# A decoder megakernel: one section per layer of its local-attention network, and 4-bit rounding from exponent bits

## The chip, the cores and the metric

The kernel runs on one core of a Trainium2 chip. The metric is the time of one execution on the device in microseconds (us); lower is better. The engines of a core are TensorE (PE; its weight loads are PEld), VectorE (DVE), ScalarE (ACT), GpSimd (POOL) and SyncE (SP), which issues DMAs.

## What is computed

Twelve stages in a row form a decoder: four layers of self-attention, cross-attention and a feed-forward part, on x of 4 x 256 tokens of width 128, all in float32. The change touches two of them.

The feed-forward part of layer 2 (`l2_ffn`) multiplies values that are rounded to a 4-bit grid in blocks of 16:

```python
_GRID = [0.0, 0.5, 1.0, 1.5, 2.0, 3.0, 4.0, 6.0]
_MID = [0.25, 0.75, 1.25, 1.75, 2.5, 3.5, 5.0]
scale = max(max(abs(xb)) / 6.0, 1e-12)           # over each block of 16
idx = searchsorted(_MID, abs(xb / scale))
q = _GRID[idx] * sign(xb) * scale
```

The last stage (`l3_ffn`) is a network of 6 layers of its own. Each layer shifts half of the channels by one token, projects to q, k and v for 16 heads of width 64, brings each head's q and k to unit length (a square, a sum over 64, a root, a reciprocal, a product), rotates them by position, attends within a local window (each block of 64 queries sees 96 keys at most), multiplies the heads by an output matrix and adds that; then follow a second shift, a layer norm and a gated feed-forward part.

## The kernel before

Every stage is a sequence of sections. A section (`nc.Block`) holds one program per engine, and at its end all engines wait for each other. Inside, engines are ordered by semaphores alone, and each engine works through its own program in the order written. A PSUM bank holds 128 x 512 float32. There are eight.

*The quantizer* (`quantize` in `l2_ffn`) is called twice, for a tile of 128 x 2144 (weights and tokens) and for one of 128 x 2816 (hidden values). ScalarE makes magnitudes and signs; VectorE then runs 14 instructions in a chain, each waiting for the one before: block maximum, scale, reciprocal, product, nine for the comparison with the seven midpoints, the doubling, and the sign (lines 1716 to 1723), and the product with the scale (line 1725).

*One pass of the layer loop* in `l3_ffn` (from line 1848) has these sections: transpose and shift; `project`; `local_attention`; the output product (`chunk_block` with the tag `heads_`, line 1884); the second shift; `norm`; the gated part.

`project` (line 1956) takes 16 steps u: 2 halves of the 1024 columns by 8 tiles of 128 tokens. In each, TensorE makes q, k and v, 128 x 512 each (lines 2012 and 2017; q and k go round six banks, v round two); ScalarE squares q and k into the two-deep buffer `squares` (2029; it shares its memory with `flat_p`, so the profile calls it `net_probs_turned`), takes the root of the step before (2034) and copies v (120); VectorE sums the squares (2059), takes the reciprocal of the step before (2064), guards this step's sum against zero (2068), and scales q and k of the step before into `unit` (2074). SP loads the layer's other weights and copies parts of v to `mid`. GpSimd has nothing to do.

`local_attention` (line 2076) works on 32 groups g (8 pairs of heads by 4 batches) in a software pipeline: GpSimd makes sine products (2152), TensorE transposes q and k and their sine products (2214, 2223), VectorE adds the two (2257, 2264), TensorE makes the scores on top of a window mask (2170, 2175), VectorE the maximum (2253), ScalarE the exponential with its sum (2237), GpSimd the division (2159), TensorE transposes (2188), VectorE copies (122), TensorE multiplies with the values (2203), ScalarE stores (120). On TensorE each turn of the loop is: scores of g, transposes of the probabilities of g-2, head products of g-3, transposes of g+3.

## Time and profile before

| | us |
|---|---|
| runs, median of 3 (lowest to highest) | 3107.61 (3104.6 to 3107.93) |
| profiled execution, own time | 3099.19 |
| its span | 3097.4 |
| TensorE busy | 2685.4 (87%) |
| VectorE busy | 1887.1 (61%) |
| ScalarE busy | 1459.9 (47%) |
| GpSimd busy | 993.8 (32%) |

The profile is one execution, with times counted from the span's start. The page gives sums over all twelve stages, which have different limits; a table of stretches or the timeline tells what one stage does. In the second pass of the layer loop `project` runs from about 2057 to 2108, the attention to about 2215, and the output product to 2231. The mean granted TensorE clock over the span is 0.937 of full speed.

### The profile page before, as it was taken

The numbers are of one execution on the slowest core, as the hardware profiler recorded it, in microseconds if no ns is written. First come the engines' busy times: TensorE is split into PE (matmuls) and PEld (weight loads), VectorE is DVE, ScalarE is ACT, GpSimd is POOL, SyncE is SP. The second block draws the span as 40 slices with busy tenths as digits, with TensorE's granted clock in tenths as the row PEclk, the third lists the DMA queues.
The fourth block names the chain that finished last, engine by engine and source line by source line (L and its number), as shares of the span: only waits on it lengthen the run. The fifth ranks groups of instructions, "written<-read, shape, count | busy, mean of one in ns | idle before, by whom it ended". The sixth has DMA issues, their size and how long they took to land. (4 is left out here: it accounts for less than half of the span.)

```text
span 3097.4 us, 61372 instructions
## 1 busy us (share of the span) xinstructions
PE 2685.4 (87%) x20645; PEld 1724.8 (56%) x20645; DVE 1887.1 (61%) x4110; ACT 1459.9 (47%) x4871; POOL 993.8 (32%) x1103
## 2 busy tenths in 40 slices
PE   5899969789899799672799979989989899899898
PEld 3555546456465465451455545746747647567376
DVE  3566656456577455557455558758578487486674
ACT  1455537227577365221355545445445355353543
POOL 0344425005366133000144423505306125043061
PEclk8899979899899899885899989999999999999999
DMA  2000000000000000000000011010010010100100
GB/s 65 1 0 0 0 8 2 26 19 2 4 1 2 30 0 0 5 8 0 26 1 0 0 49 28 2 53 12 22 42 2 30 34 2 49 15 22 42 2 28
DMA packets 42002, 49.32 MB, mean 16 GB/s; under 512 B 11963, under 2 KB 31301, under 8 KB 40838
## 3 DMA queue, kind: packets, MB, share of 16 engines
q1 hardware_dynamic: 41734, 45.89, 5.1%
q8 instruction: 151, 2.47, 0.3%
q14 instruction: 117, 0.96, 0.1%
HBM read 32.76 MB, written 0.52 MB: 11 GB/s over the span
## 5 line engine op out<-in xcount | busy, mean ns | idle before, releaser
L2152 POOL TENSOR_TENSOR net_sin_rows<-net_unit_qk,net_sin_table 128x512 f32<-128x512 f32 x192 | 243.1, 1269 | 680.4 <-SPq L2106 505.5
L2237 ACT ACTIVATE net_probs<-scores,net_negmax 128x96 f32<-128x96 f32 x768 | 251.7, 340 | 291.8 <-DVE net_negmax L2253 291.8
L1019 POOL TENSOR_TENSOR l_probs<-l_probs,rowinv 128x512 f32<-128x512 f32 (+2 forms) x256 | 192.3, 772 | 600.1 <-DVE rowinv L1031 599.3
L1039 DVE TENSOR_REDUCE negmax<-scores 128x1 f32<-128x508 f32 (+4 forms) x512 | 213.0, 468 | 221.7 <-PE scores L916 179.5
L1019 POOL TENSOR_TENSOR lora_probs<-lora_probs,rowinv 128x508 f32<-128x508 f32 (+1 forms) x256 | 149.5, 617 | 251.2 <-DVE rowinv L1031 251.2
L984 ACT ACTIVATE l_probs<-scores,negmax 128x512 f32<-128x512 f32 (+2 forms) x256 | 139.7, 552 | 166.9 <-DVE negmax L1039 166.2
L122 DVE COPY turned<-flip 128x512 f32<-128x512 f32 (+3 forms) x280 | 163.3, 583 | 74.1 <-PE flip L943 65.7
L2012 PE MATMUL bank<-net_w_qkv,xnT 128*128 128x512 f32 x384 | 199.6, 644 | 6.4 <-PEq L1848 6.4
L731 DVE TENSOR_REDUCE negmax<-scores 128x2 f32<-128x256 f32 (+2 forms) x192 | 157.8, 822 | 61.4 <-PE scores L639 34.9
L916 PE MATMUL scores<-kT,qM 64*128 64x512 f32 (+2 forms) x768 | 186.4, 562 | 9.1 <-ACT kT L120 4.7
L984 ACT ACTIVATE lora_probs<-scores,negmax 128x508 f32<-128x508 f32 (+1 forms) x256 | 117.9, 473 | 130.5 <-DVE negmax L1039 130.5
L2159 POOL TENSOR_TENSOR net_probs<-net_probs,net_inverse 128x384 f32<-128x384 f32 x192 | 158.2, 824 | 51.7 <-DVE net_inverse L2276 51.7
L2253 DVE TENSOR_REDUCE net_negmax<-scores 128x4 f32<-128x384 f32 x192 | 106.7, 556 | 105.0 <-PE scores L2175 105.0
L120 ACT ACTIVATE turned<-flip 128x512 f32<-128x512 f32 (+3 forms) x280 | 143.5, 513 | 56.9 <-PE flip L653 46.4
L966 PE MATMUL heads<-turned,V 128*64 128x256 f32 (+1 forms) x1280 | 166.3, 381 | 2.0 <-ACT turned L120 1.4
L2175 PE MATMUL scores<-net_qk_T 64*64 64x96 f32 (+1 forms) x3072 | 159.2, 243 | 0.0
L2214 PE MATMUL turn<-ident,net_unit_qk 128*128 128x128 f32 x768 | 129.7, 293 | 30.7 <-PEq L1973 30.7
L2237 ACT ACTIVATION_READ_ACCUMULATOR net_probs<-scores,net_negmax 128x1 f32 x768 | 156.1, 203 | 0.0
L2029 ACT ACTIVATE net_probs_turned<-bank 128x512 f32<-128x512 f32 x192 | 113.9, 597 | 81.8 <-PE bank L2012 81.8
L2175 PEld LDWEIGHTS scores<-net_qk_T 64*64 64x64 f32 x3072 | 123.0, 133 | 49.6 <-issue 49.6
L2264 DVE TENSOR_TENSOR net_qk_T<-turn,net_cos_T 128x512 f32<-128x512 f32 x192 | 132.8, 692 | 11.8 <-PE turn L2223 5.4
L716 POOL TENSOR_TENSOR cross_probs<-cross_probs,rowinv 128x1024 f32<-128x1024 f32 x64 | 119.8, 1893 | 61.6 <-DVE rowinv L726 61.6
(404 smaller groups left out, 6173.2 us busy)
## 6 DMA issues: line engine op xcount, KB each, us to landing
net_w_qkv<-in_L_ffn_Wqkv SPq DMA_DIRECT2D x7, 1536.0 KB, 6.2
net_vals_between<-net_vals SPq DMA_DIRECT2D x48, 192.0 KB, 2.5
net_w_out<-in_L_ffn_Wo SPq DMA_DIRECT2D x6, 512.0 KB
net_vals_between<-net_vals SPq DMA_DIRECT2D x48, 64.0 KB, 1.9
moe_w<-in_L_ffn_w13T SPq DMA_DIRECT2D x8, 256.0 KB, 2.7
net_w<-in_L_ffn_W SPq DMA_DIRECT2D x6, 341.0 KB
moe_w<-in_L_ffn_w2T SPq DMA_DIRECT2D x8, 128.0 KB, 2.3
ctx_tok<-in_ctx SPq DMA_DIRECT2D x1, 768.0 KB, 6.6
```

The lines of the kernel that those rows point to most:

```text
L122: return nc.vector.tensor_copy(dst, src)
L731: nc.vector.tensor_reduce(negmax[:, c:c + 2], scores[:, 2 * half:2 * half + 2, 0:nk], AX.X, ALU.max, negate=True).then_inc(maxed.sem, 1)
L916: last = nc.tensor.matmul(scores[:, 2 * qt + h, 0:nk], qM[rows, 0, t * P:(t + 1) * P], kT[rows, k0:k0 + nk], start=True, stop=cross)
L966: last = nc.tensor.matmul(heads[rows, q0 * P:QT * P], V[:, v0 + j, rows], turned[:, 2 * p + h, c0:c0 + w], start=(j == 0), stop=(j == part ...
L984: last = nc.scalar.activation(pr[:, slot(g, qt, h), k0:k1], scores[:, 2 * qt + h, k0:k1], ACT.Exp, bias=negmax[:, u * tail + w:u * tail + ...
L1019: last = nc.gpsimd.tensor_tensor(own, own, rowinv[:, u * tail + w:u * tail + w + 1].to_broadcast([P, k1 - k0]), ALU.mult)
L1039: last = nc.vector.tensor_reduce(negmax[:, u * tail + w:u * tail + w + 1], scores[:, 2 * qt + h, k0:k1], AX.X, ALU.max, negate=True)
L2012: nc.tensor.matmul(qk_bank(u, s), own, w_qkv[:, s * INNER + c * BANK:s * INNER + (c + 1) * BANK], start=True, stop=True).then_inc(filled.s ...
L2152: nc.gpsimd.tensor_tensor(halves(sin_rows[:, g % 2, :, :, :]), halves(tiles_of_group(g))[:, :, ::-1, :], sin_table[:, :, :, :, :].rearrang ...
L2159: nc.gpsimd.tensor_tensor(prob_blocks(g), prob_blocks(g), part, ALU.mult).then_inc(shared.sem, 1)
L2175: last = nc.tensor.matmul(scores[rows_of(h), g % 2, first:(w + 1) * KEYS], qk_T[rows_of(h), g % 3, 0, w * QB:(w + 1) * QB], qk_T[rows_of(h ...
L2237: last = nc.scalar.activation(prob_blocks(g)[:, w, :], score_blocks(g)[:, w, :], ACT.Exp, bias=maxima[:, g % 4, w:w + 1], accum_out=sums[: ...
```

## The change

The quantizer keeps the sign in the value. The value divided by the block's scale is masked to its exponent bits, which gives the power of two below it; that is held at 1 at least and multiplied by 1.5 x 2^22; adding and subtracting the result rounds the value to the grid's step. The sign instruction of ScalarE and its buffer go.

`project`, `local_attention` and the output product become one section, `attend`. k is copied from PSUM to `unit` by ScalarE; GpSimd squares it there and later scales it in place; q stays with ScalarE (square) and VectorE (scaling). The v products of TensorE and their copies follow three steps behind q and k. The attention's loops follow in the same programs, with waits for the units of a group (`wait_units`) before its sine products and its transposes, and with banks shared by hand. The output product is made in four parts, one per batch, behind the last groups; the wait for the layer's loads moves from VectorE's start of the attention to TensorE's first output part. ScalarE runs one small exponential ahead of the attention.

The removed loops of `project` and the loops of the attention that stay as they were are left out of the diff; both stand in the kernel above.

```diff
@@ quantize @@
-        STEPS = 14
-        step, side = signal("fp4_step", STEPS), signal("fp4_sign", 2)
+        STEPS = 9
+        step, side = signal("fp4_step", STEPS), signal("fp4_magnitude", 1)
         with nc.Block() as block:
             @block.scalar
             def _(act):
                 nc.scalar.activation(mag[:, 0:width], v, ACT.Abs).then_inc(side.sem, 1)
-                nc.scalar.activation(sgn[:, 0:width], v, ACT.Sign).then_inc(side.sem, 1)
             @block.vector
             def _(dve):
...
                 then(nc.vector.tensor_reduce(amax[:, 0:nb], blocks(mag), AX.X, ALU.max))
                 then(nc.vector.tensor_scalar(amax[:, 0:nb], amax[:, 0:nb], 1.0 / 6.0, 1e-12, ALU.mult, ALU.max))
                 then(nc.vector.reciprocal(inv[:, 0:nb], amax[:, 0:nb]))
-                then(nc.vector.tensor_tensor(blocks(mag), blocks(mag), of_block(inv), ALU.mult))
-                dve.wait_ge(side.sem, side.at(0, 2))
-                then(nc.vector.tensor_scalar(v, m, 5.0, 2.0, ALU.is_gt, ALU.mult))
-                then(nc.vector.scalar_tensor_tensor(v, m, 3.5, v, ALU.is_gt, ALU.add))
-                then(nc.vector.scalar_tensor_tensor(v, m, 2.5, v, ALU.is_gt, ALU.add))
-                then(nc.vector.tensor_scalar(v, v, 2.0, None, ALU.mult))
-                for mid in (1.75, 1.25, 0.75, 0.25):
-                    then(nc.vector.scalar_tensor_tensor(v, m, mid, v, ALU.is_gt, ALU.add))
-                then(nc.vector.scalar_tensor_tensor(v, v, 0.5, sgn[:, 0:width], ALU.mult, ALU.mult))
                 v3 = v.rearrange("p (n k) -> p n k", k=FP4_BLOCK)
+                then(nc.vector.tensor_tensor(v3, v3, of_block(inv), ALU.mult))
+                then(nc.vector.tensor_scalar(m.bitcast(I32), v.bitcast(I32), EXPONENT, None, ALU.bitwise_and))
+                then(nc.vector.tensor_scalar(m, m, 1.0, HALF_STEPS, ALU.max, ALU.mult))
+                then(nc.vector.scalar_tensor_tensor(v, v, 1.0 - 2.0 ** -24, m, ALU.mult, ALU.add))
+                then(nc.vector.tensor_tensor(v, v, m, ALU.subtract))
                 then(nc.vector.tensor_tensor(v3, v3, of_block(amax), ALU.mult))
                 assert done[0] == STEPS
...
@@ l3_ffn, layer loop @@
-        project(l, p, unit, vals, mid, mid_in, w_qkv, squares, norms, (sines, sin_table, cosines, cos_table, qk_rows, qk_cols),
-                loaded, (vec, w1, w2, w_out, GT))
-        local_attention(l, loaded, NLOADS, unit, vals, mid, mid_in, sin_table, cos_table, sin_rows, cos_T, qk_T, probs, flat_p,
-                        (maxima, sums, inverse), window16)
-        chunks = []
-        for t in (0, 4):
-            def outs(o, t=t):
-                for q in range(4):
-                    for c in range(PAIRS):
-                        last = nc.tensor.matmul(o[:, q * D:(q + 1) * D], unit[:, c, t + q, 0, :],
-                                                w_out[:, c, :], start=(c == 0), stop=(c == PAIRS - 1))
-                return last
-            chunks.append(Chunk("dve", outs, add_to(xin, t)))
-        chunk_block(chunks, n=l, iters=DEPTH, tag="heads_")
+        attend(l, p, unit, vals, mid, (sines, sin_table, cosines, cos_table, qk_rows, qk_cols), (sin_rows, cos_T, qk_T),
+               (squares, norms), (probs, flat_p, maxima, sums, inverse, window16), (loaded, NLOADS),
+               (vec, w_qkv, w1, w2, w_out, GT))
...
@@ attend (was project and local_attention) @@
+QK_BANKS, V_BANKS = (2, 3, 4, 5, 0, 1), (6, 7)
+TURN_BANKS, SCORE_BANKS, FLIP_BANKS, HEADS_BANK = (QK_BANKS[2], QK_BANKS[3], V_BANKS[0]), (QK_BANKS[4], QK_BANKS[5]), QK_BANKS[0:2], V_BANKS[1]
+OUT_BANKS = TURN_BANKS + SCORE_BANKS[0:1]
...
+    def wait_units(eng, g):
+        c, b = group(g)
+        for made in united:
+            eng.wait_ge(made.sem, made.at(l, c * D // BANK * NT + QT * (b + 1)))
...
@@ gpsimd @@
+        def make_sines(g):
+            if g >= 2:
+                pool.wait_ge(turned_sin.sem, turned_sin.at(l, g - 1))
+            wait_units(pool, g)
+            nc.gpsimd.tensor_tensor(halves(sin_rows[:, g % 2, :, :, :]), halves(tiles_of_group(g))[:, :, ::-1, :],
+                                    sin_table[:, :, :, :, :].rearrange("p t s h (f d) -> p (t s h) f d", f=2),
+                                    ALU.mult).then_inc(sined.sem, 1)
+        for u in range(STEPS + 1):
+            if u < STEPS:
+                pool.wait_ge(k_copied.sem, k_copied.at(l, u + 1))
+                if u >= 2:
+                    pool.wait_ge(added.sem, added.at(l, u - 1))
+                own = own_rows(unit, u, 1)
+                nc.gpsimd.tensor_tensor(by_pair(squares[:, u % 2, 1, :]), own, own, ALU.mult).then_inc(squared[1].sem, 1)
+            if u == STEPS:
+                pool.wait_ge(tabled.sem, tabled.at(l, 6))
+                make_sines(0)
+            if u >= 1:
+                own = by_head(own_rows(unit, u - 1, 1))
+                pool.wait_ge(norms_in.sem, norms_in.at(l, u))
+                nc.gpsimd.tensor_tensor(own, own, factors(u - 1, 1), ALU.mult).then_inc(united[1].sem, 1)
+        for s in range(1 - SINES, G + NORM):
             g = s + SINES
             if 0 <= g < G:
-                if g >= 2:
-                    pool.wait_ge(turned_sin.sem, turned_sin.at(l, g - 1))
-                nc.gpsimd.tensor_tensor(halves(sin_rows[:, g % 2, :, :, :]), halves(tiles_of_group(g))[:, :, ::-1, :],
-                                        sin_table[:, :, :, :, :].rearrange("p t s h (f d) -> p (t s h) f d", f=2),
-                                        ALU.mult).then_inc(sined.sem, 1)
+                make_sines(g)
...
@@ tensor @@
+        for u in range(STEPS + LATE_V):
+            if u < STEPS:
+                c, t = half_of(u)
+                for s, free in ((0, united[0]), (1, k_copied)):
+                    if u >= len(QK_BANKS) // 2:
+                        pe.wait_ge(free.sem, free.at(l, u - len(QK_BANKS) // 2 + 1))
+                    nc.tensor.matmul(qk_bank(u, s), xnT[:, t * P:(t + 1) * P],
+                                     w_qkv[:, s * INNER + c * BANK:s * INNER + (c + 1) * BANK],
+                                     start=True, stop=True).then_inc(filled.sem, 1)
+            v = u - LATE_V
+            if v >= 0:
+                c, t = half_of(v)
+                if v >= len(V_BANKS):
+                    pe.wait_ge(v_copied.sem, v_copied.at(l, v - len(V_BANKS) + 1))
+                nc.tensor.matmul(v_bank(v), xnT[:, t * P:(t + 1) * P], w_qkv[:, 2 * INNER + c * BANK:2 * INNER + (c + 1) * BANK],
+                                 start=True, stop=True).then_inc(v_filled.sem, 1)
...
+                wait_units(pe, g)
...
+            b = s - VALUES - LAST - 1
+            if b >= 0:
+                pe.wait_ge(stored.sem, stored.at(l, LAST + b + 1))
+                if b == 0:
+                    pe.wait_ge(loaded.sem, loaded.at(l, nloads))
+                    pe.wait_ge(rotated.sem, rotated.at(l, G))
+                    pe.wait_ge(exped.sem, exped.at(l, G))
+                for q in range(QT):
+                    for c in range(PAIRS):
+                        last = nc.tensor.matmul(out_bank(b)[:, q * D:(q + 1) * D], unit[:, c, QT * b + q, 0, :], w_out[:, c, :],
+                                                start=(c == 0), stop=(c == PAIRS - 1))
+                last.then_inc(out_made.sem, 1)
...
@@ scalar @@
+        for u in range(STEPS + LATE_V):
+            if u < STEPS:
+                act.wait_ge(filled.sem, filled.at(l, 2 * u + 1))
+                if u >= 2:
+                    act.wait_ge(added.sem, added.at(l, u - 1))
+                nc.scalar.activation(squares[:, u % 2, 0, :], qk_bank(u, 0), ACT.Square).then_inc(squared[0].sem, 1)
+                act.wait_ge(filled.sem, filled.at(l, 2 * u + 2))
+                copy("act", own_rows(unit, u, 1), by_pair(qk_bank(u, 1))).then_inc(k_copied.sem, 1)
+            if 1 <= u <= STEPS:
+                act.wait_ge(guarded.sem, guarded.at(l, u))
+                own = norms[:, (u - 1) % 2, :, :]
+                nc.scalar.activation(own, own, ACT.Sqrt).then_inc(rooted.sem, 1)
+            v = u - LATE_V
+            if v >= 0:
+                c, t = half_of(v)
+                act.wait_ge(v_filled.sem, v_filled.at(l, v + 1))
+                copy("act", vals[:, t, c * BANK:(c + 1) * BANK], v_bank(v)).then_inc(v_copied.sem, 1)
+        nc.scalar.activation(primer[:, :], ones[:, 0:1], ACT.Exp).then_inc(primed.sem, 1)
...
@@ vector @@
+        for u in range(STEPS + 1):
+            if u < STEPS:
+                for made in squared:
+                    dve.wait_ge(made.sem, made.at(l, u + 1))
+                if u >= 2:
+                    for made in united:
+                        dve.wait_ge(made.sem, made.at(l, u - 1))
+                nc.vector.tensor_reduce(norms[:, u % 2, :, :], squares[:, u % 2, :, :].rearrange("p s (h d) -> p s h d", d=DH),
+                                        AX.X, ALU.add).then_inc(added.sem, 1)
+            if u >= 1:
+                own = norms[:, (u - 1) % 2, :, :]
+                dve.wait_ge(rooted.sem, rooted.at(l, u))
+                nc.vector.reciprocal(own, own).then_inc(norms_in.sem, 1)
+            if u < STEPS:
+                own = norms[:, u % 2, :, :]
+                dve.wait_ge(added.sem, added.at(l, u + 1))
+                nc.vector.tensor_scalar(own, own, 1e-24, None, ALU.max).then_inc(guarded.sem, 1)
+            if u >= 1:
+                dve.wait_ge(norms_in.sem, norms_in.at(l, u))
+                nc.vector.tensor_tensor(by_head(own_rows(unit, u - 1, 0)), by_head(by_pair(qk_bank(u - 1, 0))), factors(u - 1, 0),
+                                        ALU.mult).then_inc(united[0].sem, 1)
...
+        for b in range(B):
+            own = xin[:, QT * b:QT * (b + 1), :]
+            dve.wait_ge(out_made.sem, out_made.at(l, b + 1))
+            nc.vector.tensor_tensor(own, own, out_bank(b).rearrange("p (t d) -> p t d", t=QT), ALU.add).then_inc(out_added.sem, 1)
```

## Rows read from the trace of the kernel before

**Rows 1.** The page: busy time, share of the span and instructions of each engine.
```profile
PE 2685.4 (87%) x20645; PEld 1724.8 (56%) x20645; DVE 1887.1 (61%) x4110; ACT 1459.9 (47%) x4871; POOL 993.8 (32%) x1103
```

**Rows 2.** Projection, mid-attention: us; PE, PEld, DVE, ACT, POOL busy (count); clock, DMA, GB/s.
```profile
2057.00:2108.40 51.40, 46.30 (x96) 17.82 (x96) 45.03 (x86) 31.40 (x65) 0.00 (x0) 0.93 0.23 62
2125.30:2197.30 72.00, 72.00 (x944) 57.84 (x943) 58.15 (x116) 38.54 (x208) 47.27 (x46) 1.00 0.01 2
```

**Rows 3.** Timeline, start of the projection: start, length, engine, line, operation [idle before <-releaser].
```profile
2060.87 0.60 ACT L2029 ACTIVATE net_probs_turned<-bank 128x512 f32<-128x512 f32 x1 [1.11 <-PE bank L2012]
...
2061.94 0.60 ACT L120 ACTIVATE net_vals<-bank 128x512 f32<-128x512 f32 x1 [0.47 <-PE bank L2017]
...
2062.80 0.60 ACT L2029 ACTIVATE net_probs_turned<-bank 128x512 f32<-128x512 f32 x1 [0.26 <-PE bank L2012]
...
2064.29 1.22 DVE L2059 TENSOR_REDUCE net_qk_norms<-net_probs_turned 128x16 f32<-128x1024 f32 x1 [1.36 <-ACT net_probs_turned L2029]
```

**Rows 4.** Timeline, one steady step of the projection.
```profile
2073.13 1.22 DVE L2059 TENSOR_REDUCE net_qk_norms<-net_probs_turned 128x16 f32<-128x1024 f32 x1
...
2074.27 0.24 DVE L2064 RECIPROCAL net_qk_norms<-net_qk_norms 128x16 f32<-128x16 f32 x1
...
2074.43 0.13 DVE L2068 TENSOR_SCALAR net_qk_norms<-net_qk_norms 128x16 f32<-128x16 f32 x1
...
2074.55 1.29 DVE L2074 TENSOR_TENSOR net_unit_qk<-bank,net_qk_norms 128x512 f32<-128x512 f32 x2
...
2075.29 0.30 PEld L2012 LDWEIGHTS bank<-net_w_qkv,xnT 128*128 128x128 f32 x2 [0.79 <-DVE net_unit_qk L2074]
```

**Rows 5.** Timeline, last sum of squares, GpSimd's first sines, first window product.
```profile
2103.99 1.22 DVE L2059 TENSOR_REDUCE net_qk_norms<-net_probs_turned 128x16 f32<-128x1024 f32 x1
...
2108.48 3.79 POOL L2152 TENSOR_TENSOR net_sin_rows<-net_unit_qk,net_sin_table 128x512 f32<-128x512 f32 x3 [84.91 <-SPq L2106]
...
2113.25 0.33 PE L2170 MATMUL scores<-net_window,ident 128*128 128x384 bf16 x1
```

**Rows 6.** GpSimd's groups by shape, two of them.
```profile
L2152 POOL TENSOR_TENSOR net_sin_rows<-net_unit_qk,net_sin_table 128x512 f32<-128x512 f32 x192 | 243.1, 1269 | 680.4 <-SPq L2106 505.5 <-PE turn L2223 174.8
...
L1019 POOL TENSOR_TENSOR l_probs<-l_probs,rowinv 128x512 f32<-128x512 f32 x128 | 130.3, 1039 | 445.4 <-DVE rowinv L1031 445.4
```

**Rows 7.** Timeline, hand-overs from VectorE to GpSimd to TensorE.
```profile
2208.96 0.18 DVE L2276 RECIPROCAL net_inverse<-net_sums 128x4 f32<-128x4 f32 x1 [0.87 <-ACT net_probs L2237]
...
2209.22 0.83 POOL L2159 TENSOR_TENSOR net_probs<-net_probs,net_inverse 128x384 f32<-128x384 f32 x1 [1.26 <-DVE net_inverse L2276]
...
2210.10 0.42 PEld L2188 LDWEIGHTS flip<-ident,net_probs 128*128 128x128 f32 x4 [0.18 <-POOL net_probs L2159]
```

**Rows 8.** TensorE's queue: a separate wait (ns), and idle time before head products.
```profile
L2220 PEldq EVENT_SEMAPHORE  x186: 51/51/51, 1901.9 to 3035.4; - x186
...
2126.68 0.20 PEld L2203 LDWEIGHTS heads<-net_probs_turned,net_vals 128*64 128x64 f32 x4 [0.17 <-issue]
```

**Rows 9.** Timeline, last head products, last copy, output products, last addition.
```profile
2211.44 0.44 PE L2203 MATMUL heads<-net_probs_turned,net_vals 128*64 128x128 f32 x4 [0.68 <-ACT net_unit_qk L120]
...
2214.73 0.38 ACT L120 ACTIVATE net_unit_qk<-heads 128x256 f32<-128x256 f32 x1 [0.85 <-PE heads L2203]
...
2215.42 14.53 PE L1884 MATMUL bank<-net_w_out,net_unit_qk 128*128 128x128 f32 x128 [0.73 <-PEq L2106]
...
2229.99 0.69 DVE L490 TENSOR_TENSOR xin<-xin,bank 128x512 f32<-128x512 f32 x1 [6.46 <-PE bank L1884]
```

**Rows 10.** Timeline, the quantizer's rounding steps, first and last of both calls.
```profile
1389.51 1.28 DVE L1716 TENSOR_SCALAR fp_inputs<-fp_mag 128x2144 f32<-128x2144 f32 x1
...
1409.11 2.39 DVE L1725 TENSOR_TENSOR fp_inputs<-fp_inputs,fp_amax 128x2144 f32<-128x2144 f32 x1
...
1437.90 1.63 DVE L1716 TENSOR_SCALAR fp_hid<-fp_mag 128x2816 f32<-128x2816 f32 x1
...
1463.11 3.09 DVE L1725 TENSOR_TENSOR fp_hid<-fp_hid,fp_amax 128x2816 f32<-128x2816 f32 x1
```

345 lines of the change are left out of this document (168 added, 177 removed).

## The prediction, made before the changed kernel ran

> **What bounds the kernel now.** I read the page first: TensorE is busy for 87% of the span, no other engine for more than 61% [rows 1]. That average covers twelve stages, and the change touches two places, so the stretches of those decide. The table by stretch of the layer loop's second pass (of six) [rows 2] shows two regimes. In the projection (51.4 us) VectorE is busy for 45.0 us and TensorE for 46.3 us at a mean clock of 0.93; in the middle of the attention (72.0 us) TensorE is busy all the time at the full clock and VectorE for 58.2 us. So in the attention a TensorE instruction costs its time, and work of the others is hidden.
>
> The timeline of one projection step [rows 4] says who sets the pace: VectorE starts the sum of squares at 2073.13, the reciprocal 1.14 us later, the guard 0.16 after that, the two scalings 0.12 after that, and the next sum 1.39 later: 2.81 us with no hole. TensorE waits 0.79 us for a scaling to free a bank. From the sum of step 1 at 2064.29 [rows 3] to that of step 15 at 2103.99 [rows 5] there are 14 periods in 39.70 us, 2.84 each. GpSimd does nothing in this stretch. In the 4-bit quantizer [rows 10] VectorE runs alone, one instruction after another, each waiting for the last: all of it is on the path.
>
> **The quantizer.** Between the normalization by the block maximum and the last product stand now two one-input instructions and seven with two inputs. For the 2144 wide call they fill 1389.51 to 1409.11, 19.60 us; for the 2816 wide one 1437.90 to 1463.11, 25.21 us. Two one-input and two two-input instructions replace them. One-input ones take 1.28 and 1.63 us, two-input ones 2.39 and 3.09 us, each with some 0.03 between: 2 x 1.31 + 2 x 2.42 = 7.5 us and 2 x 1.66 + 2 x 3.12 = 9.6 us. Saved: 12.1 + 15.6 = 27.8 us. The mask on integers isn't in the trace. If it ran at the two-input pace it would cost 1.1 and 1.5 us more (saved 25.2); a gain below the one-input row is not to be had for as many elements. I take the row of the same kind, 27.8. The sign on ScalarE ran beside VectorE's first reduction: worth nothing.
>
> **The projection, step by step.** VectorE loses one scaling of two (about 0.65 us), so by itself it would need some 2.2 us a step; TensorE would then be next, with 46.3 / 16 = 2.9 us a step at 0.93 of the clock (2.7 at the full one). But the new order makes a ring through two engines. GpSimd issues in program order: square k(u), wait for the reciprocal of u-1, scale k(u-1), square k(u+1). VectorE issues: wait for both squares of u, sum(u), and only then the reciprocal of u-1. So the square of u releases the sum of u, behind it comes the reciprocal of u-1, that releases the scaling of u-1, and behind this waits the square of u+1. None of the four overlaps another. Double buffers don't help, since it is queue order that ties them. The period is:
> - sum to reciprocal, start to start: 1.14 [rows 4];
> - reciprocal 0.24 [rows 4] and the hand-over to GpSimd 0.08 (reciprocal ends 2209.14, GpSimd starts 2209.22) [rows 7]: 0.32;
> - scaling 128x512 on GpSimd with a factor repeated over 64 elements: the nearest row is the scaling of 128x512 probabilities by a repeated factor, 1.04 [rows 6];
> - square 128x512: not in the trace as such. Bounds: 1.04, the row with a repeated operand, and 1.27, the row with two full 512 wide operands [rows 6]. It reads two full streams (the same one twice): I take 1.27;
> - hand-over back: 0.05, as from GpSimd to TensorE (2210.05 to 2210.10) [rows 7].
>
> Sum 3.82 us a step, against 2.84. Guard, q's scaling (done 2.1 us after the sum's start), ScalarE's square, copy, root and copy (some 2.0 us) and TensorE's products lie inside it: bank waits are for step u-3 and k is copied before it is wanted, so they have over 1 us to spare. 14 periods take 53.5 instead of 39.7 us: +13.8 per pass. With the square at 1.04 the period is 3.59 and the price 10.6; with both at 1.27 it is 4.05 and 17.0. A sum gets three waits more on VectorE's queue, a few hundredths, left to the range.
>
> The Trainium skill (GPSIMD Engine Reference, section 3.1) gives a GpSimd instruction with two inputs about 2.6 cycles per element and dispatch on top, and section 4.1 says to keep elementwise work on VectorE. The rows agree for two full operands but show 1.04 for a repeated one; if the page's rule held for the scaling too, the time would be 6 x 3.2 = 19 us above my sum. By both the work moved is dearer where it lands.
>
> **Start of the projection.** k's first copy ends at 2061.47. Value products go behind, so k1 takes the place that q1 has now (2062.80) [rows 3]: copied at 2063.40, squared from 2063.48 to 2064.75, sum of step 1 at 2064.80 instead of 2064.29: +0.5 (+0.3 with the quicker square).
>
> **The seam to the attention.** Now the first window product of the scores comes at 2113.25, 9.26 us after the last sum's start (2103.99) [rows 5]; the barrier holds everybody until 2108.48, then GpSimd makes three sine products in 3.79 us. New, counted from that sum: scaling of k14 ends at 1.14 + 0.32 + 1.04 = 2.50, sines(0) at 3.77, scaling of k15 at 4.81, sines(1) at 6.08, sines(2) at 7.35, its turn and the window product at about 7.85. Gain 1.4. The last value product waits for ScalarE and is over by about 4 us, so TensorE isn't late. If TensorE is slow here, the gain is 0.9. Loading the exponential's table earlier gains nothing: ScalarE waits there for the first scores anyway.
>
> **The attention itself.** The instructions are the same. TensorE gets two more waits for every group (q and k of the group's tiles), with the group's transposes queued behind them and VectorE and ScalarE behind those. They are satisfied long before, but a wait of its own on that queue takes 0.051 us, and before the head products there is a hole of 0.17 us at such a place [rows 8]. As TensorE has no idle time there [rows 2], I take 2 x 0.051 = 0.10 us for 28 groups: +2.8 per pass. Bounds: 0, if the queue runs ahead, and 0.17, or 4.8 per pass. GpSimd's two extra waits per group are hidden by its idle time.
>
> **The end of the attention.** Now TensorE waits between the last groups and for the barrier, then makes the output product in 14.53 us from 2215.42, and the addition ends at 2230.68 [rows 9]. New, the four parts stand between the last groups: after the head products of group 29 (2211.44 to 2212.1) come three group pieces of 0.6 and the four parts, 16.3 us, to 2228.45, and a half-size addition of about 0.5 to 2229.0. Gain 1.7; bounds 0 (the parts wait for ScalarE's copies) and 2.0. What is late next is TensorE itself. SP issues the same DMAs in the same order; the wait for the layer's loads moves from VectorE to TensorE, 100 us after they were issued, so it costs nothing.
>
> **Sum.** Per pass +0.5 + 13.8 - 1.4 - 1.7 + 2.8 = +14.0, times six +84.0; less 27.8: +56. The profiled execution took 3099.2 us (span 3097.4), so 3155.4; the median of the runs is 8.4 above the profiled one, which gives 3163.8, 1.8% slower. All low ends together: 6 x (0.3 + 10.6 - 1.4 - 2.0) - 27.8 = +17, 3125. All high ends: 6 x (0.7 + 17.0 - 0.9 + 4.8) - 25.2 = +104, 3212.
>
> **Rivals.**
> 1. *Slower, but less: the extra waits are free and the square takes 1.04.* For it: most pieces of TensorE's work follow each other without a hole, though they have such waits. Against: nothing shows a full two-operand instruction at 1.04. With the seam and the end as forecast 6 x (0.3 + 10.6 - 1.4 - 1.7) - 27.8 = +19, about 3127. Chance 0.15.
> 2. *Faster: the ring isn't the limit*, because the GpSimd pair is far quicker than the nearest rows or its queue gets ahead of the reciprocal. Then TensorE bounds a step at 2.6 to 2.7: 14 x (2.6 - 2.84) = -3.3 per pass, with the rest -3.1 per pass, six times -19, less 27.8: -46, 3061. It decides at a period of 3.15 us, where the six passes just eat the quantizer's gain (84 x (p - 2.84) = 27.8 + 15.6 - 16.8); 3.35 with free waits. For it: GpSimd was idle and VectorE full. Against: the ring follows from program order, and its two GpSimd pieces would have to take 1.64 us together where the rows give 2.08 at the least. Chance 0.11.
> 3. *Slower by more: TensorE's clock.* In the ring TensorE works 2.6 of 3.8 us. At the lower of its two levels (1.2 GHz) the 2.9 us of a step become 2.9 x 0.93 x 2 = 5.4, above the ring: 14 x 1.6 = 22 per pass, +130, near 3295; a part of the steps is likelier than all. Against: it would then be busy without a pause, and in the stages of [rows 2] with few pauses the clock was 0.93 and 1.00. Chance 0.08.
>
> **Numbers.** The forecast's own case has 0.64; 0.02 is left for a sum that comes out within 0.2%, about what a measurement of this kernel can tell from no change (6 us). Slower 0.87, same 0.02, faster 0.11. Range 3120 to 3200: rival 1 is in, rival 2 and most of rival 3 are out.
>
> **What would show it.** In the changed profile: sums of squares 3.8 us apart, each ended by a wait for GpSimd; GpSimd waiting for the reciprocal in the projection; VectorE's busy share in that stretch down to about 60%; four VectorE instructions instead of nine in each quantizer call; group periods of the attention 3.2 instead of 3.13 us. Sums 2.8 us apart or less would make the prediction wrong; so would a square of 0.6 us.

## The result: 3125.3 us, 0.6% slower

The changed kernel takes 3125.32 us (median of 4 runs, 3123.1 to 3126.39), the kernel before, run beside it, 3106.11 us; the ratio is 1.0063 with a 95% interval of 1.0046 to 1.0081. The forecast was 3164, +56 us; what came is +19 us by the medians and +25.1 us between the two profiled executions (3124.31 against 3099.19; spans 3122.5 and 3097.4). The time lies inside the stated range, at its low end, and the direction and the mechanism came as forecast; the size did not.

The page of the changed kernel, first its busy times (to be held against [rows 1]), then four groups of the projection (columns: line, engine, operation, count | busy us, mean ns of one | idle before, and what ended most of it):

```profile
PE 2706.1 (87%) x20645; PEld 1726.7 (55%) x20645; DVE 1802.9 (58%) x4016; ACT 1457.7 (47%) x4875; POOL 1190.9 (38%) x1295
...
L2087 POOL TENSOR_TENSOR net_sin_rows<-net_unit_qk,net_sin_table 128x512 f32<-128x512 f32 x192 | 243.4, 1272 | 172.1 <-PE bank L2216 172.1
...
L2292 DVE TENSOR_REDUCE net_qk_norms<-net_probs_turned 128x16 f32<-128x1024 f32 x96 | 117.1, 1220 | 150.9 <-POOL net_probs_turned L2098 146.6
...
L2098 POOL TENSOR_TENSOR net_probs_turned<-net_unit_qk 128x512 f32<-128x512 f32 x96 | 99.9, 1041 | 228.7 <-ACT net_unit_qk L122 228.7
...
L2106 POOL TENSOR_TENSOR net_unit_qk<-net_unit_qk,net_qk_norms 128x512 f32<-128x512 f32 x96 | 100.1, 1043 | 139.3 <-DVE net_qk_norms L2297 139.3
```

VectorE is busy 84 us less, GpSimd 197 us more, and the kernel is slower. The two lines that say why are the second and the fourth: the sums of squares wait 146.6 us for GpSimd's square, and the 96 scalings on GpSimd wait 139.3 us for VectorE's reciprocal. Two engines that wait for each other are a ring. The third line has the surprise: the square takes 1.041 us, not 1.27 as the sines do.

One turn of the ring, VectorE's and GpSimd's timelines of the second pass (start, length, engine, line, operation, and in brackets the idle time before it with its releaser). It answers to [rows 4]:

```profile
2059.32 1.22 DVE L2292 TENSOR_REDUCE net_qk_norms<-net_probs_turned 128x16 f32<-128x1024 f32 x1 [1.48 <-POOL net_probs_turned L2098]
2060.46 0.24 DVE L2297 RECIPROCAL net_qk_norms<-net_qk_norms 128x16 f32<-128x16 f32 x1
2060.62 0.13 DVE L2301 TENSOR_SCALAR net_qk_norms<-net_qk_norms 128x16 f32<-128x16 f32 x1
2060.74 0.69 DVE L2304 TENSOR_TENSOR net_unit_qk<-bank,net_qk_norms 128x512 f32<-128x512 f32 x1
2062.91 1.22 DVE L2292 TENSOR_REDUCE net_qk_norms<-net_probs_turned 128x16 f32<-128x1024 f32 x1 [1.49 <-POOL net_probs_turned L2098]
...
2060.78 1.04 POOL L2106 TENSOR_TENSOR net_unit_qk<-net_unit_qk,net_qk_norms 128x512 f32<-128x512 f32 x1 [1.55 <-DVE net_qk_norms L2297]
2061.78 1.04 POOL L2098 TENSOR_TENSOR net_probs_turned<-net_unit_qk 128x512 f32<-128x512 f32 x1
```

Sum at 2059.32, reciprocal 1.14 later, scaling 0.32 later, square 1.00 later, next sum 1.13 later: 3.59 us. The forecast put 1.14, 0.32, 1.04 and 1.27 + 0.05 in these places. With 1.04 for the square it gives 3.59 as well: the scaling holds the queue 0.04 less and the way from the square to the sum is 0.04 more, which cancels.

The stretch of the fourteen periods and one in mid-attention, as [rows 2] has them for before (us; PE, PEld, DVE, ACT, POOL busy with counts; clock, DMA, GB/s):

```profile
2048.30:2098.80 50.50, 40.30 (x82) 15.07 (x82) 29.48 (x57) 26.12 (x57) 28.62 (x28) 0.97 0.12 32
2112.00:2184.00 72.00, 71.68 (x934) 57.52 (x934) 58.08 (x116) 38.46 (x210) 47.39 (x46) 1.00 0.01 2
```

VectorE is down to 29.48 of 50.50 us (58%), TensorE to 80%, and nobody is full: that is how a stage looks that is limited by a ring of waits.

The quantizer's new steps, VectorE's timeline of both calls; they answer to [rows 10]:

```profile
1393.21 1.28 DVE L1717 TENSOR_SCALAR fp_mag<-fp_inputs 128x2144 int32<-128x2144 int32 x1
1394.52 1.28 DVE L1718 TENSOR_SCALAR fp_mag<-fp_mag 128x2144 f32<-128x2144 f32 x1
1395.83 2.39 DVE L1720 SCALAR_TENSOR_TENSOR fp_inputs<-fp_inputs,fp_mag 128x2144 f32<-128x2144 f32 x1
...
1400.68 2.39 DVE L1722 TENSOR_TENSOR fp_inputs<-fp_inputs,fp_amax 128x2144 f32<-128x2144 f32 x1
...
1431.40 1.63 DVE L1717 TENSOR_SCALAR fp_mag<-fp_hid 128x2816 int32<-128x2816 int32 x1
...
1440.98 3.09 DVE L1722 TENSOR_TENSOR fp_hid<-fp_hid,fp_amax 128x2816 f32<-128x2816 f32 x1
```

7.47 us where 19.60 stood and 9.58 where 25.21 stood: 27.8 us saved, as forecast, with the mask on integers at 1.28 us, the pace of the one-input row.

Not all of it arrives. Between the end of the first call and the block maximum of the second, where TensorE works, 18.58 us became 20.52. The two stretches with their first 9 us, before and after (columns as in [rows 2]):

```profile
1411.50:1420.50 9.00, 7.64 (x30) 5.85 (x31) 2.35 (x7) 4.07 (x7) 0.00 (x0) 0.75 0.00 0
1411.50:1430.08 18.58, 13.49 (x49) 9.27 (x49) 6.00 (x14) 8.51 (x13) 0.00 (x0) 0.87 0.00 0
...
1403.07:1412.07 9.00, 7.63 (x24) 5.74 (x25) 1.81 (x6) 3.27 (x5) 0.00 (x0) 0.50 0.00 0
1403.07:1423.59 20.52, 15.70 (x49) 10.56 (x49) 6.01 (x15) 8.61 (x12) 0.00 (x0) 0.75 0.00 0
```

In both kernels TensorE had been idle through the first call (0.00 us busy from 1380.0 to 1411.5 before, from 1384.0 to 1403.0 after). In the 9 us behind it the granted clock was 0.75 before and 0.50, the lower level, after. The same holds in all eleven profiles with the new quantizer: 0.50 in those 9 us, 20.2 to 20.7 us for the stretch. So 1.6 to 2.1 us of the 27.8 are given back at once. Why the clock came back sooner before is not shown.

The seam and the end of the attention in the same pass (they answer to [rows 5] and [rows 9]):

```profile
2098.79 1.22 DVE L2292 TENSOR_REDUCE net_qk_norms<-net_probs_turned 128x16 f32<-128x1024 f32 x1 [1.48 <-POOL net_probs_turned L2098]
...
2101.25 1.27 POOL L2087 TENSOR_TENSOR net_sin_rows<-net_unit_qk,net_sin_table 128x512 f32<-128x512 f32 x1
...
2103.47 4.97 POOL L2087 TENSOR_TENSOR net_sin_rows<-net_unit_qk,net_sin_table 128x512 f32<-128x512 f32 x4
...
2106.55 0.33 PE L2148 MATMUL bank<-net_window,ident 128*128 128x384 bf16 x1
...
2107.68 0.56 DVE L2310 TENSOR_REDUCE net_negmax<-bank 128x4 f32<-128x384 f32 x1 [1.03 <-PE bank L2153]
...
2149.94 0.83 PE L2153 MATMUL bank<-net_qk_T 64*64 64x64 f32 x16
...
2153.07 0.67 PE L2153 MATMUL bank<-net_qk_T 64*64 64x64 f32 x12
...
2221.95 0.42 DVE L2337 TENSOR_TENSOR xin<-xin,bank 128x256 f32<-128x256 f32 x1 [3.15 <-PE bank L2229]
```

From the last sum to the first window product 7.76 us (7.85 forecast, 9.26 before). A group still takes 3.13 us (2149.94 to 2153.07): the extra waits on TensorE cost nothing that shows. From the first score maximum to the end of the last addition 114.69 us in every pass; before it was 116.29.

### The profile page after: what moved, and what is told of

It is laid out like the page before. It is cut to its first block and busy times, and to the rows that moved or that the text cites. A ratio compares the mean times of both kernels' runs of the same rounds, so it can differ in the third digit from the quotient of the medians.

```text
span 3122.5 us, 61628 instructions
## 1 busy us (share of the span) xinstructions
PE 2706.1 (87%) x20645; PEld 1726.7 (55%) x20645; DVE 1802.9 (58%) x4016; ACT 1457.7 (47%) x4875; POOL 1190.9 (38%) x1295
## 5 line engine op out<-in xcount | busy, mean ns | idle before, releaser
L2263 ACT ACTIVATE net_probs<-bank,net_negmax 128x96 f32<-128x96 f32 x768 | 251.7, 340 | 284.0 <-DVE net_negmax L2310 284.0
L2292 DVE TENSOR_REDUCE net_qk_norms<-net_probs_turned 128x16 f32<-128x1024 f32 x96 | 117.1, 1220 | 150.9 <-POOL net_probs_turned L2098 146.6
L2098 POOL TENSOR_TENSOR net_probs_turned<-net_unit_qk 128x512 f32<-128x512 f32 x96 | 99.9, 1041 | 228.7 <-ACT net_unit_qk L122 228.7
L2126 PEld LDWEIGHTS bank<-net_w_qkv,xnT 128*128 128x128 f32 x384 | 72.3, 205 | 195.8 <-DVE net_unit_qk L2304 125.6
L122 ACT ACTIVATE net_unit_qk<-bank 128x256 f32<-128x256 f32 (+1 forms) x288 | 132.9, 462 | 81.3 <-PE bank L2186 55.6
L2310 DVE TENSOR_REDUCE net_negmax<-bank 128x4 f32<-128x384 f32 x192 | 106.7, 556 | 106.7 <-PE bank L2153 106.7
L2153 PE MATMUL bank<-net_qk_T 64*64 64x96 f32 (+1 forms) x3072 | 159.2, 243 | 0.0
L2263 ACT ACTIVATION_READ_ACCUMULATOR net_probs<-bank,net_negmax 128x1 f32 x768 | 156.0, 203 | 0.0
L2106 POOL TENSOR_TENSOR net_unit_qk<-net_unit_qk,net_qk_norms 128x512 f32<-128x512 f32 x96 | 100.1, 1043 | 139.3 <-DVE net_qk_norms L2297 139.3
```

What stands on the lines that cost most here:

```text
L122: return nc.scalar.activation(dst, src, ACT.Copy, scale=scale)
L2126: nc.tensor.matmul(qk_bank(u, s), xnT[:, t * P:(t + 1) * P], w_qkv[:, s * INNER + c * BANK:s * INNER + (c + 1) * BANK], start=True, stop=T ...
L2153: last = nc.tensor.matmul(bank[rows_of(h), SCORE_BANKS[g % 2], first:(w + 1) * KEYS], qk_T[rows_of(h), g % 3, 0, w * QB:(w + 1) * QB], qk_ ...
L2263: last = nc.scalar.activation(prob_blocks(g)[:, w, :], score_blocks(g)[:, w, :], ACT.Exp, bias=maxima[:, g % 4, w:w + 1], accum_out=sums[: ...
```

## Where the time went

One number separates the layer loop from all ahead of it: the start of the loop's first sum of squares. Before, it is at 1852.85 of a span of 3097.4, so the loop's part is 1244.6 us; after, at 1831.16 of 3122.5: 1291.3 us. So +46.8 in the loop and -21.7 ahead of it, in sum +25.1. The -21.7 are +3.7 ahead of the quantizer (its first block maximum starts at 1387.07, before at 1383.37), -25.8 from there to the end of the second call, and +0.4 behind it. The loop's part repeats between kernels that have the same loop (1244.6 before and 1244.7 with the new quantizer alone), the start of the loop does not: 1829.4 to 1844.6 over eleven kernels whose instructions up to there are the same. Most of that scatter is there before the quantizer, whose first block maximum starts between 1384.5 and 1398.4. The experiments are therefore read by the loop's part, and their times beside it.

## Experiments

All times are medians of 4 to 10 runs; "after" is the changed kernel. The loop's part and the 14 periods (from the sum of step 1 to that of step 15, mean of the six passes) are from one profiled execution each. The kernel before, run beside them, took 3104.7 us beside the new quantizer alone, one section, two more waits and square ahead of scaling; 3104.4 beside the two kernels with norms three deep; 3103.4 beside the other four.

| kernel | us | ratio to before [95%] | loop's part | 14 periods |
|---|---|---|---|---|
| before | 3106.1 | 1 | 1244.6 | 39.7 |
| after | 3125.3 | 1.0063 [1.0046, 1.0081] | 1291.3 | 50.3 |
| new quantizer alone | 3079.0 | 0.9920 [0.9899, 0.9942] | 1244.7 | 39.7 |
| one section, old engines | 3057.3 | 0.9837 [0.9812, 0.9861] | 1221.1 | 40.0 |
| two more waits | 3132.0 | 1.0082 [1.0056, 1.0108] | 1292.4 | 50.2 |
| other operand | 3151.6 | 1.0156 [1.0132, 1.0180] | 1312.6 | 53.5 |
| scaling alone on GpSimd | 3049.6 | 0.9826 [0.9809, 0.9842] | 1212.4 | 38.1 |
| square ahead of scaling | 3128.6 | 1.0079 [1.0061, 1.0098] | 1293.4 | 50.8 |
| the same, norms three deep | 3087.5 | 0.9946 [0.9931, 0.9962] | 1248.6 | 42.9 |
| norms three deep alone | 3127.3 | 1.0081 [1.0054, 1.0108] | 1291.5 | 50.3 |
| reciprocal first | 3104.7 | 0.9996 [0.9986, 1.0006] | 1264.4 | 44.4 |
| reciprocal and q first | 3078.4 | 0.9916 [0.9899, 0.9932] | 1244.0 | 40.6 |

### The parts one by one

**New quantizer alone**: the kernel before with the whole new quantizer (four rounding steps, the sign kept in the value, ScalarE's sign instruction gone) and nothing else.

```
-then(nc.vector.tensor_scalar(v, m, 5.0, 2.0, ALU.is_gt, ALU.mult))
... (six more)
+then(nc.vector.tensor_scalar(m.bitcast(I32), v.bitcast(I32), EXPONENT, None, ALU.bitwise_and))
+then(nc.vector.tensor_scalar(m, m, 1.0, HALF_STEPS, ALU.max, ALU.mult))
+then(nc.vector.scalar_tensor_tensor(v, v, 1.0 - 2.0 ** -24, m, ALU.mult, ALU.add))
+then(nc.vector.tensor_tensor(v, v, m, ALU.subtract))
```

> The kernel before with the new quantizer alone. Theory A (the quantizer's term of the sum was right): 27.8 us less, 3078 (3075 to 3082). Rival (part of the gain is given back in the sections behind it): less than 22 us.

Measured 3079.0, 25.7 below its before; the loop's part is unchanged to 0.2 us. The quantizer's term stands, and so, in a small part, does the rival: in its profile the stretch between the two calls takes 20.66 us against 18.58, 2.1 us given back.

**One section, old engines**: the changed kernel with ScalarE squaring k from its bank and VectorE scaling it, as before.

```
-copy("act", own_rows(unit, u, 1), by_pair(qk_bank(u, 1))).then_inc(k_copied.sem, 1)
+nc.scalar.activation(squares[:, u % 2, 1, :], qk_bank(u, 1), ACT.Square).then_inc(squared[1].sem, 1)
...
+for s in range(2):
+    nc.vector.tensor_tensor(by_head(own_rows(unit, u - 1, s)), by_head(by_pair(qk_bank(u - 1, s))), factors(u - 1, s), ALU.mult)
```

> The changed kernel, but k goes as it did before: squared by ScalarE and scaled by VectorE out of PSUM, GpSimd idle in the projection. One section per layer, v three steps behind, output product in four parts and the quantizer stay. Theory A: the step is back at 2.84 us or a little less, the seam and the end keep their gains of 1.4 to 2.5 and 1.6 us: 27.8 + 6 x (3.0 to 4.1) = 46 to 52 us below the kernel before: 3054 to 3060. Rival (the single section itself is what costs, by v's products behind or by the waits): 3078 or more, what the quantizer alone gives.

Measured 3057.3. The 14 periods are 40.0 us (39.7 before), the seam takes 7.85 us from the last sum to the first maximum (10.35 as the mean of before's passes) and the attention's 114.69. Merging the sections is a gain of 23.5 us, and the 70.2 us by which after's loop is longer than this one all come with the two pieces moved to GpSimd: 61.5 in the 14 periods of the six passes, 6 in the seams.

### The two terms that were mis-sized

**Two more waits**: two satisfied waits more in TensorE's program for each of 30 groups, 60 in a pass.

```
 if g >= 2:
+    pe.wait_ge(v_copied.sem, v_copied.at(l, STEPS))
+    pe.wait_ge(k_copied.sem, k_copied.at(l, STEPS))
```

> The changed kernel with two more waits (for v's and k's copies, long satisfied) ahead of the transposes of every group from the third on, on top of the two that the change added. Theory A (TensorE's queue runs ahead of its array there, a satisfied wait is hidden): group period 3.13 us, time as the changed kernel, 3125. Rival (each wait costs its 0.05 us and the first two were hidden by a small reserve that is now used up): 3.23 us a group, +3 us per pass, +18: 3143.

The first score maximum and the last addition of its first pass:

```profile
1897.68 0.56 DVE L2313 TENSOR_REDUCE net_negmax<-bank 128x4 f32<-128x384 f32 x1 [1.38 <-PE bank L2153]
...
2011.95 0.42 DVE L2340 TENSOR_TENSOR xin<-xin,bank 128x256 f32<-128x256 f32 x1 [3.15 <-PE bank L2232]
```

2012.37 less 1897.68 is 114.69 us, the same as without them. Not every wait of the program shows as an instruction of its own. In the trace of after, `wait_units` leaves 32 separate waits a pass on the weight-load queue (L2027), one a group; here the lines of `wait_units` and of the new waits have 61, two a group from the fourth on, 51 ns each. Neither the 32 nor the 29 on top of them cost anything that shows, so the forecast's 2.8 us a pass was wrong. The median is 6.7 us above after's, but the loop's part only 1.1; the rest lies ahead of the loop, where nothing was changed.

**Other operand**: GpSimd multiplies k by a table instead of by itself; the norms of k are then no norms, the amount of work is the same.

```
-nc.gpsimd.tensor_tensor(by_pair(squares[:, u % 2, 1, :]), own, own, ALU.mult)
+nc.gpsimd.tensor_tensor(by_pair(squares[:, u % 2, 1, :]), own, by_pair(cosines[:, :, :].rearrange("p s n -> p (s n)")), ALU.mult)
```

> Change: GpSimd's product for k's squares reads the cosine table as its second operand instead of k a second time, so the norms of k are no norms (this part of the computation is changed, nothing else). Open: in the changed kernel the square of 128x512 took 1.041 us, the product of rotated halves of the same size 1.272. Theory A, it costs more to read two different tensors than one tensor twice: the square takes 1.27, the period goes from 3.59 to 3.82 us, 14 x 6 x 0.23 = +19 us, so 3144. Theory B, the 1.27 comes from the short reversed runs (32 wide) of the rotated halves: the square stays at 1.04, the period at 3.59, and the time at 3125 (the changed kernel's).

GpSimd's timeline in the projection:

```profile
2076.84 1.04 POOL L2106 TENSOR_TENSOR net_unit_qk<-net_unit_qk,net_qk_norms 128x512 f32<-128x512 f32 x1 [1.55 <-DVE net_qk_norms L2297]
2077.84 1.27 POOL L2098 TENSOR_TENSOR net_probs_turned<-net_unit_qk,net_cosines 128x512 f32<-128x512 f32 x1
2080.66 1.04 POOL L2106 TENSOR_TENSOR net_unit_qk<-net_unit_qk,net_qk_norms 128x512 f32<-128x512 f32 x1 [1.55 <-DVE net_qk_norms L2297]
```

Theory A holds: with two different tensors read in full the same product takes 1.27 us, with one tensor twice 1.04. (The scaling's second tensor is a factor repeated over 64 elements, and it takes 1.04 as well.) The short reversed runs of the sines have no part in it. The period is 3.82 us (2076.84 to 2080.66), to the hundredth what the prediction had worked out with 1.27, and the loop's part is 21.2 us longer (19 expected). So the ring was right as a sum of terms; one term had the price of another operand pattern.

### Is it the ring, and which order breaks it

**Scaling alone on GpSimd**: ScalarE squares k from the bank and copies it; GpSimd loses the square and keeps the scaling.

```
+nc.scalar.activation(squares[:, u % 2, 1, :], qk_bank(u, 1), ACT.Square).then_inc(squared[1].sem, 1)
 copy("act", own_rows(unit, u, 1), by_pair(qk_bank(u, 1))).then_inc(k_copied.sem, 1)
```

> Change: ScalarE squares k from the bank and then copies it; GpSimd has only the scaling of k in the projection. Ring theory (the period is the way from square to sum to reciprocal to scaling to square): without the square in GpSimd's queue no ring of that kind is left; the next limits are TensorE at 2.6 to 2.7 us a step and ScalarE's queue (square, square, copy, root, value copy), some 2.6. Period 2.6 to 2.8, 14 x 6 x (3.59 - 2.7) = -75 us, so 3040 to 3060; at or below the version with one section and the old engines (3057). Rival, GpSimd as such costs it (each hand-over to it and back, wherever it stands): the period stays over 3.2 and the time over 3090. Rival 2: ScalarE, with one more instruction a step and its waits for the banks, becomes the limit at 3.0 or more: 3075 and over.

Two sums of one pass in its timeline, with the scaling that ends the wait of the second:

```profile
2051.01 1.22 DVE L2287 TENSOR_REDUCE net_qk_norms<-net_probs_turned 128x16 f32<-128x1024 f32 x1 [0.53 <-POOL net_unit_qk L2100]
...
2052.47 1.04 POOL L2100 TENSOR_TENSOR net_unit_qk<-net_unit_qk,net_qk_norms 128x512 f32<-128x512 f32 x1 [1.59 <-DVE net_qk_norms L2292]
...
2053.21 1.94 PE L2120 MATMUL bank<-net_w_qkv,xnT 128*128 128x512 f32 x4
...
2053.64 1.22 DVE L2287 TENSOR_REDUCE net_qk_norms<-net_probs_turned 128x16 f32<-128x1024 f32 x1 [0.53 <-POOL net_unit_qk L2100]
```

The period is 2.63 us, below before's 2.84, and the limit is now TensorE, which is busy in all of the last eleven periods of the second pass at the full clock (columns as in [rows 2]):

```profile
2048.37:2077.34 28.97, 28.97 (x68) 11.71 (x66) 23.17 (x45) 25.02 (x58) 11.47 (x11) 1.00 0.19 51
```

Both rivals fall: a hand-over to GpSimd and back in every step is no obstacle when no second piece of GpSimd's stands in the ring, and ScalarE bears the extra square. The loop's part is 79 us shorter than after's (75 expected). At 3049.6 us this is the fastest kernel of the study, 1.7% below before; its loop is 8.7 us shorter than with the old engines.

**Square ahead of scaling**: GpSimd squares u+1 before it scales u-1.

```
-if u < STEPS:
-    pool.wait_ge(k_copied.sem, k_copied.at(l, u + 1))
+for v in ([0, 1] if u == 0 else [u + 1] if u + 1 < STEPS else []):
+    pool.wait_ge(k_copied.sem, k_copied.at(l, v + 1))
```

> The changed kernel with one thing moved on GpSimd: the square of k for step u+1 stands before the scaling of step u-1 instead of behind it. No instruction is added or taken away. Theory A (the step's length is a ring through two queues: square, sum, reciprocal, scaling, square): the ring now spans two steps, so a step falls from 3.59 us to what TensorE's six products need, 2.6 to 2.9 us; 14 x 0.7 to 1.0 = 10 to 14 us per pass, 60 to 84 us in all: 3041 to 3065, below both kernels. Rival (GpSimd or VectorE is slow in itself, or the two get in each other's way): the same work, so the step stays at 3.6 and the time at 3125.

A miss: 3128.6 us, no gain. Two steps of its timeline:

```profile
2077.56 1.22 DVE L2292 TENSOR_REDUCE net_qk_norms<-net_probs_turned 128x16 f32<-128x1024 f32 x1 [2.38 <-POOL net_unit_qk L2106]
...
2079.73 1.98 PE L2126 MATMUL bank<-net_w_qkv,xnT 128*128 128x512 f32 x4 [1.65 <-DVE net_unit_qk L2304]
2080.19 1.22 DVE L2292 TENSOR_REDUCE net_qk_norms<-net_probs_turned 128x16 f32<-128x1024 f32 x1 [0.52 <-POOL net_unit_qk L2106]
...
2081.75 0.60 ACT L122 ACTIVATE net_unit_qk<-bank 128x512 f32<-128x512 f32 x1 [0.18 <-PE bank L2126]
...
2082.51 1.04 POOL L2098 TENSOR_TENSOR net_probs_turned<-net_unit_qk 128x512 f32<-128x512 f32 x1 [2.44 <-ACT net_unit_qk L122]
...
2083.50 1.04 POOL L2106 TENSOR_TENSOR net_unit_qk<-net_unit_qk,net_qk_norms 128x512 f32<-128x512 f32 x1
...
2084.68 1.22 DVE L2292 TENSOR_REDUCE net_qk_norms<-net_probs_turned 128x16 f32<-128x1024 f32 x1 [2.38 <-POOL net_unit_qk L2106]
```

The sums now wait for the scaling (L2106), not the square. The norms are two deep, so sum(u) waits for the scaling of k(u-2); this stands behind square(u) in GpSimd's queue; and that waits for the new k, whose product TensorE makes behind q's, in a bank that is freed by the scaling of q(u-3), which VectorE makes behind sum(u-2). From sum(u-2) to sum(u), 2077.56 to 2084.68, it is 7.12 us for two steps, 3.56 each. I had taken one ring away and had not looked for the next. The reading was then tested:

**The same, norms three deep**, and **norms three deep alone** (the changed kernel, nothing else).

```
-norms = sbl("qk_norms", [P, 2, 2, BANK // DH])
+norms = sbl("qk_norms", [P, 3, 2, BANK // DH])
...
-if u >= 2:
+if u >= 3:
     for made in united:
-        dve.wait_ge(made.sem, made.at(l, u - 1))
+        dve.wait_ge(made.sem, made.at(l, u - 2))
```

> Change: as the kernel with GpSimd's square of u+1 ahead of its scaling of u-1, and the norms three deep instead of two, so that the sum of u waits for the scaling of u-3 and no longer for that of u-2. My reading of that earlier kernel (two steps take 7.12 us since sum(u) waits for the scaling of k(u-2), which stands behind square(u)): with the third buffer this wait is gone and what is left is the ring by the banks (scaling of q(u-1), products of u+2, k's copy, square, sum), 6.0 to 6.2 us for two steps: period 3.0 to 3.1, 84 x (3.55 - 3.05) = -42 us, so about 3080 to 3090. Rival, GpSimd's order never mattered (it paces by its own load and hand-overs): period stays at 3.5 to 3.6, 3125 to 3130.

> Change: the changed kernel with the norms three deep instead of two, nothing else. Ring theory: queue order ties the square, the sum, the reciprocal and the scaling, not the buffer; the period stays 3.59 and the time 3125. Rival, the buffer of the norms is what couples the steps in the changed kernel as well: the period falls below 3.4 and the time to 3105 or less.

Both as expected. With both edits two steady steps take 6.06 to 6.07 us, the 14 periods 42.5 to 43.6 us in the six passes (3.07 each in the mean), and the loop's part is 44.8 us below that of square first alone (42 expected) and 42.7 below after's. The third buffer alone gives 50.3 us and a loop of 1291.5: nothing. In the changed kernel the order of the queues binds and the buffer does not; with the order mended the buffer binds.

**Reciprocal first**, and **reciprocal and q first**: on VectorE the reciprocal of u-1, or that and the scaling of q(u-1), ahead of the sum of u.

```
+if u >= 1:
+    own = norms[:, (u - 1) % 2, :, :]
+    dve.wait_ge(rooted.sem, rooted.at(l, u))
+    nc.vector.reciprocal(own, own).then_inc(norms_in.sem, 1)
 ... (second kernel: the scaling of q(u-1) here too)
 nc.vector.tensor_reduce(norms[:, u % 2, :, :], ...)
```

> Change: on VectorE the reciprocal of step u-1 stands ahead of the sum of squares of step u, nothing else. Ring theory: the scaling of k(u-1) no longer waits for sum(u), so the square of u and that scaling lie beside the sum. What is left is a longer ring by the banks (scaling of q(u-1), products of u+2, k's copy, square, sum), and VectorE's own 2.2 us: period 2.8 to 3.0, 84 x (3.59 - 2.9) = -58 us, so 3060 to 3075. Rival, the pace is GpSimd's own load (square and scaling, 2.08 us, and two hand-overs): then the order on VectorE is nothing and the time stays at 3125. Rival 2: the reciprocal, now first, exposes ScalarE's root of the step before and the period is above 3.3: over 3100.

> Change: on VectorE the reciprocal of step u-1 and the scaling of q(u-1) both stand ahead of the sum of squares of step u. Ring theory: the bank of q is freed a sum earlier than with the reciprocal alone first, so the ring by the banks is shorter by 1.1 us; the root of u-1 has had no instruction of VectorE's to hide behind but the guard, so VectorE waits for it (copy, root: some 0.3 to 0.6 us a step): period 2.6 to 3.0, 84 x (3.59 - 2.8) = -66, so 3045 to 3075, and at most as much as with the reciprocal alone first. Rival, the exposed root costs a whole second latency: period 3.3 and over, 3100 and over. Rival 2, GpSimd's own load paces: 3125.

A steady step of the second:

```profile
2072.12 1.21 DVE L2300 TENSOR_REDUCE net_qk_norms<-net_probs_turned 128x16 f32<-128x1024 f32 x1
...
2073.37 0.52 DVE L2305 TENSOR_SCALAR net_qk_norms<-net_qk_norms 128x16 f32<-128x16 f32 x1
...
2073.92 0.21 ACT L2248 ACTIVATE net_qk_norms<-net_qk_norms 128x16 f32<-128x16 f32 x1 [1.26 <-DVE net_qk_norms L2305]
...
2074.17 0.25 DVE L2288 RECIPROCAL net_qk_norms<-net_qk_norms 128x16 f32<-128x16 f32 x1 [0.28 <-ACT net_qk_norms L2248]
...
2074.45 0.69 DVE L2291 TENSOR_TENSOR net_unit_qk<-bank,net_qk_norms 128x512 f32<-128x512 f32 x1
...
2075.06 1.21 DVE L2300 TENSOR_REDUCE net_qk_norms<-net_probs_turned 128x16 f32<-128x1024 f32 x1
```

The second came 3.4 us above the upper end of 3045 to 3075, at 3078.4: its period is 2.94 us, and GpSimd is in it no longer. It is the sum of VectorE's own pieces and the root it now waits for (1.25 to the guard, 0.55 to the root, 0.25, 0.28, 0.61 to the next sum). The loop's part is 47.3 us below after's, where 66 were expected. The first missed its range by 30 us. Its steady pace is as expected, 2.99 us (steps of 2.6 to 2.7 and 3.3 to 3.4 in turn), but every pass has one step of 5.2 to 5.4 us at its start, which makes 44.4 us of the 14 periods, and a seam 0.7 to 0.8 us longer; the loop's part falls by 26.9 us and not by 58. That is 31 us of the 37 by which the median lies above 3125 - 58; the other 6 lie ahead of the loop. The order on VectorE matters, against the rival that GpSimd's load of 2.08 us sets the pace.

The stretches show what the long step is. In the second pass, the step ahead of it and the long step itself (columns as in [rows 2]):

```profile
2059.14:2062.29 3.15, 0.15 (x1) 0.15 (x2) 3.04 (x6) 0.98 (x3) 2.04 (x2) 1.00 0.00 0
2062.29:2067.62 5.33, 5.33 (x9) 2.26 (x10) 2.24 (x4) 1.90 (x4) 2.17 (x3) 0.68 0.00 0
```

All six banks of q and k are full, so TensorE stands idle for 3.65 us, until VectorE has scaled the first q (2062.14). Then it is busy without a pause at a mean granted clock of 0.68, that is, mostly at its lower level, and the next k comes late. It is so in all six passes (0.14 to 0.15 us busy, then a clock of 0.68 to 0.73).

## Why the prediction was wrong in size

By its own terms, per pass, forecast and measured:

| term | forecast | measured | by |
|---|---|---|---|
| ring, 14 periods | +13.8 (3.82 us) | +10.6 (3.59 us) | timelines, other operand |
| extra waits on TensorE | +2.8 | 0 | group period 3.13, two more waits |
| seam | -1.4 | -1.5 | timelines |
| end of the attention | -1.7 | -1.6 | 114.69 against 116.29 |
| start | +0.5 | +0.3, what the sum leaves | |
| quantizer, once | -27.8 | -27.8 in its instructions, 1.6 to 2.1 given back | timelines, quantizer alone |

- *What bounds the kernel* was right: the projection is paced by waits between engines, the attention by TensorE (71.68 of 72.00 us at a clock of 1.00).
- *The ring* was right in every link, and so was its consequence, that double buffers don't help (norms three deep alone: 1291.5 against 1291.3). The failed step is "It reads two full streams (the same one twice): I take 1.27". The row of the sines reads two different tensors; the square reads one twice, and takes 1.041 us. The kernel with another operand gives 1.27 and the forecast's 3.82 us. Cost: 14 x 0.23 x 6 = 19.3 us.
- *The two waits*: the failed step is "I take 2 x 0.051 = 0.10 us for 28 groups". It was too high twice over: the trace has one separate wait a group, not two, and neither that one nor a second one (two more waits) lengthens the 3.13 us of a group. The bound of 0, which the prediction named, holds. That the 0.051 us of [rows 8] passes in the sequencer while TensorE still works on what it was given before fits this, but no run separates it from other reasons. Cost: 2.8 x 6 = 16.8 us.
- Taken together: 84.0 - 19.3 - 16.8 = 47.9 for the six passes, and 46.8 was measured. The start, forecast at +0.5, is what is left and too small to tell apart: from sum 0 to sum 1 it takes 1.71 us in a pass of after where TensorE's granted clock from 2 us ahead of sum 0 to sum 1 was 1.00, and 2.93 in one where it was 0.75.
- *Ahead of the loop* the instructions saved 27.8 us, the start of the loop came 21.7 us earlier. Of the 6.1 us between them 1.9 are given back between the two calls, with TensorE at its lower level; the rest is scatter of unchanged stages, 3.7 of it ahead of the quantizer.
- *The rivals.* Rival 1 was this case to 2 us (3127; the square at 1.04 and free waits), and had 0.15. Its terms are the measured ones, but a fit to 2 us is luck: taking the loop's change from the change of the median leaves 27.6 us gained ahead of the loop in after and 18.6 to 25.9 in the other ten kernels with the same code there. It deserved more than 0.15: its two halves are bounds that the prediction itself had named, and for each the trace had a witness on its side, 1.04 us for a repeated operand [rows 6] and a TensorE queue without holes in spite of waits [rows 2]. Rival 2 (faster) needed a period of 3.15 us. Rival 3 came in one step of 84 and cost 0.3 us: the clock over the 14 periods of the second pass was 0.97, with TensorE pausing 0.7 to 0.8 us in a steady step, but one step of this pass took 3.84 us, where TensorE was busy for all of it at a mean granted clock of 0.67.
- *What the Trainium skill says of GpSimd* (GPSIMD Engine Reference, section 3.1: some 2.6 cycles per element with two inputs) doesn't tell apart where the second input comes from. This case's runs do: 1.27 us with two different tensors, 1.04 with one tensor twice or with a factor repeated 64 times.
